# Rotary tables of two blocks in one VectorE operation, moved with the second residual ahead of the roots' seed

## The chip, the cores and the metric

The kernel runs on one core of a Trainium2 chip. The metric is the device time of one launch in microseconds. The engines are TensorE (PE, with its weight loads PEld), VectorE (DVE), ScalarE (ACT), GpSimd (POOL) and SyncE (SP), which issues the DMAs here. All data are float32.

## The reference, cut to what matters

The input is 2 x 1024 tokens of 128 features. A linear-attention layer comes first, then six layers of local attention and feed-forward, then a norm and a sum. The change lies in the attention of the six layers:

```python
x_in = shift_tokens(x)                         # half of the features come from the token before
q, k, v = split(x_in @ Wqkv[i])                # 16 heads of 64
q = l2norm(q) * q_scale[i];  k = l2norm(k) * k_scale[i]
q = q * cos * scale + rotate_half(q) * sin * scale
k = k * cos / scale + rotate_half(k) * sin / scale
x = local_attention(q, k, v) @ Wo[i] + x       # windows of 32, each sees itself and the one before
h = shift_tokens(x)
x = (a * gelu(gate)) @ W2[i] + b2[i] + x       # (a, gate) = layernorm(h) @ W1[i] + b1[i]
```

## The kernel before, in words

The tokens are cut into 16 blocks of 128 for each layer. Six layers make 96 blocks, worked off in 48 pairs (PAIRS); PPL = 8 pairs are a layer and PPB = 4 pairs one of the two sequences. Each engine has a function `step(m)` that is written out by hand and holds parts of the pairs m to m - 4: the projection of pair m, the attention of pair m - 1, the output projection of pair m - 2, the feed-forward norm of pair m - 3 and the feed-forward of pair m - 4. `run` (L707) writes out the first six steps (FILLED), loops over the steps 6 to 47 and writes out four more (BEHIND). So the order on each engine is fixed, and engines meet by semaphores that count up.

What VectorE does in a step (L1391 to L1433) for the pair's even block (u = 0) and odd block (u = 1):

- `tables` (L1276), once for each block at the step's begin: multiplies the cosines and sines of the block's positions (`rope`, 4 x 64 values for each token) by the layer's scales (`scales`) into `table[:, u]`, 256 elements, both inputs in SBUF.
- `turn_cos` (L1287) and `turn_sin` (L1298, two halves): multiply the projected q or k, in PSUM, by the table. They wait for the table (`tabled`) and for ScalarE's squares. GpSimd adds the two parts (L1456).
- `norm_square` (L1304), `mask` and `largest` (L1343, L1350), `sums` (L1356, L1358), `ff_gate` (L1377), `residual1` (L1364), `ff_norm` (L1371) between them.
- `find_roots` (L1307) near the end: inverse square roots of 64 head norms of q and k of both blocks and of two variances of the feed-forward norm. A first step (L1313 from the sums of squares, L1318 from the variances in PSUM), a seed by an integer operation on the bits (L1326, 67 elements), and three Newton rounds of three operations (L1330, L1333, L1336), each waiting for the one before.
- `residual2` (L1386) last: the feed-forward's output in PSUM, its bias and the kept sum `mid` into `xT`; it waits for `down_done` and signals `x_ready`.

GpSimd's order in a step (L1503): scale k of the even and q of the odd block of pair m - 1 by the roots (L1484), fold squares (L1469), scale k of the odd block, additions (L1456), subtraction of the row maxima (L1495), weighing by the inverted sums (L1500), a fold, the additions for q and k of the odd block, and last `scale_q` of the even block of pair m, which waits for the roots of the pair.

TensorE's order (L883) around the change: `ff_down` (L879) ends a step; the next one begins with transposes of probabilities (L786), a projection of q (L781), `ff_up` part 0 (L871, waits for `x_ready`), transposes of the even block's q (`turn_q`, L789 to L795, waits for `q_scaled`), the projection of k, transposes of k, `ff_up` part 1, transposes of the odd block's q (waits also for `q_turned`, the sines of the even block, as it writes the PSUM tile that they read), `ff_up` part 2 and the scores (L814). Later come the projections of v and q, the output projection (L839) and the rest.

```python
before = ROOT_OPS * m
dve.wait_ge(S["refined"], before + 2)
...
dve.tensor_scalar(root[:, :].bitcast(I32), minus_half[:, :].bitcast(I32), -0.5, GUESS,
                  ALU.mult, ALU.add).then_inc(S["refined"], 1)
```

Of the kernel before, what the change touches and what calls it, by code (L numbers as in the profile page):

```python
# [22 lines left out]
BPB = SEQ // P  # L23
NB = BATCH * BPB
# [3 lines left out]
PAIRS = STEPS // 2  # L28
PPL = NB // 2
PPB = BPB // 2  # L30
# [18 lines left out]
ROOT_OPS = 3 + 3 * NEWTON  # L49
# [5 lines left out]
def bcast(ap, axis, count):  # L55

    wide = ap.unsqueeze(axis)
    shape = list(wide.shape)
    shape[axis] = count
    return wide.broadcast_to(shape)  # L60
# [566 lines left out]
def layers(nc, weights, xT, ident, mean_w, center_w, eps):  # L627

    with ExitStack() as ctx:
        def sb(name, shape):  # L630
            return ctx.enter_context(nc.sbuf_tensor(name, shape, F32))

        def sem(name):
            return ctx.enter_context(nc.semaphore(name))
# [5 lines left out]
        window, rope, scales = weights.window, weights.rope, weights.scales  # L640


        table = sb("table", [P, 2, 4, DH])
# [48 lines left out]
        S = {name: sem(name) for name in names}  # L692
# [4 lines left out]
        LAG, FILLED, BEHIND = 2, 6, 4  # L697

        def runs(m):

            return not isinstance(m, int) or 0 <= m < PAIRS
# [2 lines left out]

            return isinstance(n, int) and n == 0

        def run(eng, step):  # L707

            for m in range(FILLED):
                step(m)  # L710
            with eng.Fori(FILLED, PAIRS) as m:
                step(m)
            for m in range(PAIRS, PAIRS + BEHIND):
                step(m)

        def pair_at(m):

            return (m % PPL) * W2 + (m % PPL) // PPB
# [552 lines left out]

        @block.vector
        def _(dve):
            def tables(n, u):

                dve.tensor_tensor(table[:, u, :, :].rearrange("p k d -> p (k d)"),  # L1276
                                  rope[:, bass.ds(n % BPB, 1), :, :].rearrange("p a k d -> p (a k d)"),
                                  scales[:, bass.ds(n // NB, 1), :, :].rearrange("p a k d -> p (a k d)"),
                                  ALU.mult).then_inc(S["tabled"], 1)

            def turn_cos(n, u, k, src, squared, turned, transposed):

                dve.wait_ge(S["tabled"], n + 1)
                dve.wait_ge(S[squared], n + 1)
                if not isinstance(n, int) or n >= 2:
                    dve.wait_ge(S[transposed], n - 1)
                dve.tensor_tensor(rot[:, u, k, :, :, :].rearrange("p h a d -> p h (a d)"),  # L1287
                                  src[:, :].rearrange("p (h d) -> p h d", h=HEADS),
                                  bcast(table[:, u, 2 * k, :], 1, HEADS), ALU.mult).then_inc(S[turned], 1)

            def turn_sin(n, u, k, src, turned, added):

                if not first(n):
                    dve.wait_ge(S[added], n)
                v = src[:, :].rearrange("p (h a d) -> p h a d", h=HEADS, a=2)
                for a in range(2):
                    sin = table[:, u, 2 * k + 1, 32 * a:32 * a + 32]
                    dve.tensor_tensor(rot_sin[:, k, :, a, :], v[:, :, 1 - a, :], bcast(sin, 1, HEADS),  # L1298
                                      ALU.mult).then_inc(S[turned], 1)
# [4 lines left out]
                dve.tensor_reduce(ss[:, (2 * u + k) * HEADS:(2 * u + k + 1) * HEADS], squares[:, k, :].rearrange("p (h a d) -> p h a d", h=HEADS, a=2)  # L1304
                                  [:, :, 0, :], AX.X, ALU.add).then_inc(S[summed], 1)

            def find_roots(m):  # L1307

                before = ROOT_OPS * m
                if runs(m):  # L1310
                    dve.wait_ge(S["q_summed"], 2 * (m + 1))
                    dve.wait_ge(S["k_summed"], 2 * (m + 1))
                    dve.tensor_scalar(minus_half[:, 0:QK_ROOTS + 1], ss[:, :],  # L1313
                                      1e-24, -0.5, ALU.max, ALU.mult)\
                       .then_inc(S["refined"], 1 if runs(m - LAG) else 2)
                if runs(m - LAG):
                    dve.wait_ge(S["var_done"], m - LAG + 1)
                    dve.tensor_scalar(minus_half[:, QK_ROOTS + 1:ROOTS], pm_norm[:, 0:2], 1e-5, -0.5, ALU.add, ALU.mult)\  # L1318
                       .then_inc(S["refined"], 1 if runs(m) else 2)
                dve.wait_ge(S["refined"], before + 2)  # L1320
                if runs(m - 1):
                    dve.wait_ge(S["q_scaled"], 2 * m)
                    dve.wait_ge(S["k_scaled"], 2 * m)
                if runs(m - LAG - 1):
                    dve.wait_ge(S["rstd_spread"], m - LAG)
                dve.tensor_scalar(root[:, :].bitcast(I32), minus_half[:, :].bitcast(I32), -0.5, GUESS,  # L1326
                                  ALU.mult, ALU.add).then_inc(S["refined"], 1)
                for i in range(NEWTON):
                    dve.wait_ge(S["refined"], before + 3 + 3 * i)
                    dve.tensor_tensor(root_t[:, :], minus_half[:, :], root[:, :], ALU.mult)\  # L1330
                       .then_inc(S["refined"], 1)
                    dve.wait_ge(S["refined"], before + 4 + 3 * i)
                    dve.tensor_tensor(root_t[:, :], root_t[:, :], root[:, :], ALU.mult)\  # L1333
                       .then_inc(S["refined"], 1)
                    dve.wait_ge(S["refined"], before + 5 + 3 * i)
                    dve.scalar_tensor_tensor(out=root[:, :], in0=root_t[:, :], scalar=1.5, in1=root[:, :],  # L1336
                                             op0=ALU.add, op1=ALU.mult).then_inc(S["refined"], 1)
# [44 lines left out]
            def residual2(m):  # L1382

                dve.wait_ge(S["down_done"], m + 1)
                at = pair_at(m) + 1
                dve.scalar_tensor_tensor(out=xT[:, bass.ds(at, W2)], in0=pm_norm[:, 0:W2],  # L1386
                                         scalar=cols[:, 2, bass.ds(m // PPL, 1)],
                                         in1=mid[:, bass.ds(at, W2)], op0=ALU.add, op1=ALU.add)\
                   .then_inc(S["x_ready"], 1)

            def step(m):  # L1391
                if runs(m):
                    tables(2 * m, 0)
                    tables(2 * m + 1, 1)
                    turn_cos(2 * m, 0, 0, r0, "q_squared", "q_turned", "qT_done")
                    turn_sin(2 * m, 0, 0, r0, "q_turned", "q_added")
                if runs(m - 4):
                    ff_gate(m - 4, 0, pm_norm)
                if runs(m):
                    turn_cos(2 * m, 0, 1, r1, "k_squared", "k_turned", "kT_done")  # L1400
                    turn_sin(2 * m, 0, 1, r1, "k_turned", "k_added")
                    norm_square(2 * m, 0, 0, "q_folded", "q_summed")
                if runs(m - 1):
                    mask(2 * m - 2, 0, r2)
                    largest(2 * m - 2, 0)
                if runs(m - 4):
                    ff_gate(m - 4, 1, pm_out)
                if runs(m - 1):
                    mask(2 * m - 1, 1, r0)
                    largest(2 * m - 1, 1)  # L1410
                    sums(2 * m - 2, 0)
                if runs(m - 4):
                    ff_gate(m - 4, 2, pm_norm)
                if runs(m):
                    norm_square(2 * m, 0, 1, "k_folded", "k_summed")
                    turn_cos(2 * m + 1, 1, 0, r1, "q_squared", "q_turned", "qT_done")
                    norm_square(2 * m + 1, 1, 0, "q_folded", "q_summed")
                if runs(m - 2):
                    residual1(m - 2)
                if runs(m - 1):  # L1420
                    sums(2 * m - 1, 1)
                if runs(m):
                    turn_sin(2 * m + 1, 1, 0, r1, "q_turned", "q_added")
                    turn_cos(2 * m + 1, 1, 1, r0, "k_squared", "k_turned", "kT_done")
                if runs(m - 3):
                    ff_norm(m - 3)
                if runs(m):
                    turn_sin(2 * m + 1, 1, 1, r0, "k_turned", "k_added")
                    norm_square(2 * m + 1, 1, 1, "k_folded", "k_summed")
                if runs(m) or runs(m - 2):  # L1430
                    find_roots(m)
                if runs(m - 4):
                    residual2(m - 4)  # L1433

            for b in range(BATCH):
                dve.memset(mid[:, b * (SEQ + 1):b * (SEQ + 1) + 1], 0.0)
# [3 lines left out]
            dve.wait_ge(S["cleared"], 1)  # L1440
            dve.wait_ge(S["tables_loaded"], 7 * 16)
            dve.sem_inc(S["x_ready"], PPL)
            run(dve, step)

        @block.gpsimd
        def _(pool):
# [206 lines left out]
```

## Time and profile before

| what | value |
|---|---|
| median of three runs | 1858.31 us (1854.05 to 1860.98) |
| the profiled execution | 1854.16 us, span 1852.3 us |
| mean granted TensorE clock | 0.972 |
| PE busy | 1673.8 us (90%) |
| DVE busy | 1562.0 us (84%) |
| POOL busy | 1488.4 us (80%) |
| ACT busy | 1219.1 us (66%) |
| tables (L1276) | 96 operations, 155.5 us |
| roots' seed (L1326) | 50 operations, 104.6 us |

The busy time of an engine says how much of the span it had an instruction running, also one that stood still behind something else. A timeline row has the start in us from the span's start, the duration, engine, line, operation, tiles and shapes; in brackets stands how long the engine had been idle before it, and what it had waited for. "x3" means that neighbouring instructions of one kind are merged. PEclk 1.00 is the full TensorE clock, 0.50 half of it.

### The profile page before, as it was taken

The page shows a single profiled execution, that of the slowest core. Times are in us where ns is not written, and L with a number is a line of the kernel's source. Part 1 is how long each engine was busy: PE and PEld are TensorE (multiplying, and loading weights), DVE is VectorE, ACT ScalarE, POOL GpSimd, SP SyncE. Part 2 cuts the span into 40 slices and gives each one's busy share as a digit, 9 for nine tenths or more (in the row PEclk, how much of TensorE's full clock was granted, in tenths as well). Part 3 has the DMA queues.
Part 4 walks back from the last instruction along what each step waited for, and adds up shares of the span by engine and source line. Part 5 has one row for each costly group of instructions (what it writes and reads, how often), then busy time and mean ns, then how long its engine had stood idle before and what let it go on. Part 6 is the DMA issues. An engine that isn't in the chain of part 4 may idle for free. (4 is left out here: it accounts for less than half of the span.)

```text
span 1852.3 us, 76505 instructions
## 1 busy us (share of the span) xinstructions
PE 1673.8 (90%) x30992; PEld 1195.4 (65%) x30992; DVE 1562.0 (84%) x2309; ACT 1219.1 (66%) x2072; POOL 1488.4 (80%) x823
## 2 busy tenths in 40 slices
PE   4957889899999999999999999999999999999985
PEld 3634566667667666676676676676666766766664
DVE  6878667898898898988989989988889989899853
ACT  3435455677777767767677777777677676777754
POOL 3568777788888888888888888888888888888851
PEclk7979889999999999999999999999999999999999
DMA  4002132121332221332212232222242223222220
GB/s 136 1 13 57 48 92 60 47 68 45 81 105 75 54 60 48 94 96 68 68 50 67 75 103 55 68 67 66 67 106 59 54 68 79 57 68 68 58 57 23
DMA packets 80697, 121.87 MB, mean 66 GB/s; under 512 B 16776, under 2 KB 29574, under 8 KB 79750
## 3 DMA queue, kind: packets, MB, share of 16 engines
q1 hardware_dynamic: 80646, 121.14, 24.9%
q8 instruction: 38, 0.62, 0.1%
q14 instruction: 13, 0.11, 0.0%
HBM read 19.36 MB, written 1.05 MB: 11 GB/s over the span
## 5 line engine op out<-in xcount | busy, mean ns | idle before, releaser
L781 PE MATMUL r<-wqkv,xs 128*128 (+1 forms) x1152 | 560.7, 618 | 13.4 <-DVE rot_sin L1298 4.3
L1484 POOL TENSOR_TENSOR rot<-rot,root 128x1024 f32<-128x1024 f32 x192 | 377.7, 1987 | 120.6 <-DVE root L1336 120.6
L1456 POOL TENSOR_TENSOR rot<-rot,rot_sin 128x1024 f32<-128x1024 f32 x192 | 451.8, 2364 | 1.6 <-DVE rot_sin L1298 1.6
L781 PEld LDWEIGHTS r<-wqkv,xs 128*128 128x128 f32 x1152 | 210.0, 195 | 213.4 <-issue 197.7
L1131 ACT ACTIVATE squares<-r 128x512 f32<-128x512 f32 x384 | 217.6, 598 | 80.5 <-PE r L781 79.3
L1287 DVE TENSOR_TENSOR rot<-r,table 128x1024 f32<-128x1024 f32 x192 | 232.8, 1213 | 21.0 <-PE r L786 9.6
L1469 POOL TENSOR_TENSOR squares<-squares 128x512 f32<-128x512 f32 x192 | 244.5, 1273 | 6.6 <-ACT squares L1131 6.5
L1500 POOL TENSOR_TENSOR probs<-probs,rinv 128x1024 f32<-128x1024 f32 x96 | 182.7, 1903 | 81.2 <-DVE rinv L1358 81.2
L1298 DVE TENSOR_TENSOR rot_sin<-r,table 128x512 f32<-128x512 f32 x384 | 242.6, 673 | 0.0
L786 PE MATMUL r<-square,rot 128*128 128x128 f32 x1536 | 208.4, 279 | 17.3 <-POOL rot L1484 11.8
L786 PEld LDWEIGHTS r<-square,rot 128*128 128x128 f32 x1536 | 169.5, 141 | 81.2 <-issue 27.5
L1495 POOL TENSOR_TENSOR sm<-sm,rowmax 128x1024 f32<-128x1024 f32 x96 | 182.6, 1902 | 45.4 <-DVE rowmax L1350 45.1
L1343 DVE TENSOR_TENSOR sm<-r,window 128x1024 f32<-128x1024 f32 x96 | 117.6, 1225 | 109.6 <-PE r L814 109.6
L1166 ACT ACTIVATE qT<-r 128x1024 f32<-128x1024 f32 x96 | 98.2, 1023 | 165.6 <-PE r L786 165.6
L871 PE MATMUL pm<-xn,w 128*128 128x256 f32 (+1 forms) x576 | 153.4, 390 | 58.4 <-DVE xT L1386 57.8
L830 PE MATMUL r<-pT,vwin 64*64 64x32 f32 x12288 | 202.9, 221 | 2.6 <-issue 2.6
L830 PEld LDWEIGHTS r<-pT,vwin 64*64 64x64 f32 x12288 | 191.7, 137 | 13.5 <-issue 12.9
L839 PE MATMUL pm<-attnT,wo 128*128 128x256 f32 x768 | 175.5, 382 | 1.2 <-issue 1.2
L839 PEld LDWEIGHTS pm<-attnT,wo 128*128 128x128 f32 x768 | 147.0, 192 | 41.2 <-issue 23.3
L1276 DVE TENSOR_TENSOR table<-rope,scales 128x256 f32 (+1 forms) x96 | 155.5, 1658 | 10.2 <-issue 10.1
L871 PEld LDWEIGHTS pm<-xn,w 128*128 128x128 f32 (+1 forms) x576 | 93.9, 180 | 107.7 <-issue 87.0
L1116 ACT ACTIVATE kT<-r 128x1024 f32<-128x1024 f32 x96 | 98.3, 1024 | 96.6 <-PE r L786 91.4
(123 smaller groups left out, 2723.2 us busy)
## 6 DMA issues: line engine op xcount, KB each, us to landing
vwin<-vtok SPq DMA_DIRECT2D x576, 128.0 KB, 2.3
vwin<-vtok SPq DMA_DIRECT2D x384, 64.0 KB, 2.0
wqkv<-in_wqkv SPq DMA_DIRECT2D x6, 1536.0 KB, 8.3
wo<-in_wo SPq DMA_DIRECT2D x6, 512.0 KB, 4.9
w<-in_w SPq DMA_DIRECT2D x6, 341.0 KB, 2.9
x<-in_x SPq DMA_DIRECT2D x4, 256.0 KB, 3.6
rope<-in_rope SPq DMA_DIRECT2D x1, 1024.0 KB
out_x<-y SPq DMA_DIRECT2D x4, 256.0 KB, 2.3
```

What stands on the lines that cost most here:

```text
L781: pe.matmul(dst[:, c * 512:(c + 1) * 512], xs1[:, u, :], w.rearrange("p a n -> p (a n)"), start=True, stop=True).then_inc(S[done], 1)
L786: last = pe.transpose(dst[:, f * P:(f + 1) * P], src[:, f * P:(f + 1) * P], ident)
L830: last = pe.matmul(dst[DH * s:DH * (s + 1), at + WIN * w:at + WIN * (w + 1)], vwin[half, u, w, 2 * i + s, :], pT[half, u, (FT // 2) * s + ...
L839: last = pe.matmul(pm_out[:, 0:W2], wo[:, f, :], attnT[:, (f % 2) * (FT // 2) + f // 2, :], start=(f == 0), stop=(f == FT - 1))
L871: last = pe.matmul(dst[0:rows, half * W2:(half + 1) * W2], w1[:, half * FF + at:half * FF + at + rows], xn2[:, :], start=True, stop=True)
L1131: last = act.activation(squares[:, k, c * 512:(c + 1) * 512], src[:, c * 512:(c + 1) * 512], ACT.Square)
L1287: dve.tensor_tensor(rot[:, u, k, :, :, :].rearrange("p h a d -> p h (a d)"), src[:, :].rearrange("p (h d) -> p h d", h=HEADS), bcast(table ...
L1298: dve.tensor_tensor(rot_sin[:, k, :, a, :], v[:, :, 1 - a, :], bcast(sin, 1, HEADS), ALU.mult).then_inc(S[turned], 1)
L1456: pool.tensor_tensor(r, r, rot_sin[:, k, :, :, :].rearrange("p h a d -> p h (a d)"), ALU.add)\
L1469: pool.tensor_tensor(halves[:, :, 0, :], halves[:, :, 0, :], halves[:, :, 1, :], ALU.add)\
L1484: pool.tensor_tensor(r, r, bcast(root[:, at:at + HEADS], 2, DH), ALU.mult)\
L1500: pool.tensor_tensor(probs[:, u, :, :], probs[:, u, :, :], bcast(rinv[:, u, :], 2, 2 * WIN), ALU.mult)\
```

## The change

`tables` is no longer called once for each block but once for each pair, in a single operation over both blocks (2 x 256 elements; the scales are read twice through a repeated axis). It is called one pair ahead: `tables(0)` before the first step, `tables(m + 1)` in step m, behind the roots' first step. `find_roots` is cut in two, `begin_roots` (L1313, L1318) and `finish_roots` (the seed and the Newton rounds). Between the two stand now the tables of the next pair and then `residual2`, which stood behind all of the roots. The count of `tabled` goes up by one for each pair, and its waits are halved accordingly. The last looped step of VectorE is written out, since it has no next pair.

```diff
-        def run(eng, step):
+        def run(eng, step, end=PAIRS):
             for m in range(FILLED):
                 step(m)
-            with eng.Fori(FILLED, PAIRS) as m:
+            with eng.Fori(FILLED, end) as m:
                 step(m)
-            for m in range(PAIRS, PAIRS + BEHIND):
+            for m in range(end, PAIRS + BEHIND):
                 step(m)
...
-            def tables(n, u):
-                dve.tensor_tensor(table[:, u, :, :].rearrange("p k d -> p (k d)"),
-                                  rope[:, bass.ds(n % BPB, 1), :, :].rearrange("p a k d -> p (a k d)"),
-                                  scales[:, bass.ds(n // NB, 1), :, :].rearrange("p a k d -> p (a k d)"),
+            def tables(m):
+                dve.tensor_tensor(table[:, :, :, :].rearrange("p u k d -> p u (k d)"),
+                                  rope[:, bass.ds((m % PPB) * 2, 2), :, :].rearrange("p a k d -> p a (k d)"),
+                                  bcast(scales[:, bass.ds(m // PPL, 1), :, :].rearrange("p a k d -> p (a k d)"), 1, 2),
                                   ALU.mult).then_inc(S["tabled"], 1)
             def turn_cos(n, u, k, src, squared, turned, transposed):
-                dve.wait_ge(S["tabled"], n + 1)
+                dve.wait_ge(S["tabled"], n // 2 + 1)
...
-            def find_roots(m):
+            def begin_roots(m):
...
+            def finish_roots(m):
+                before = ROOT_OPS * m
                 dve.wait_ge(S["refined"], before + 2)
...
             def step(m):
                 if runs(m):
-                    tables(2 * m, 0)
-                    tables(2 * m + 1, 1)
                     turn_cos(2 * m, 0, 0, r0, "q_squared", "q_turned", "qT_done")
...
                 if runs(m) or runs(m - 2):
-                    find_roots(m)
+                    begin_roots(m)
+                if runs(m + 1):
+                    tables(m + 1)
                 if runs(m - 4):
                     residual2(m - 4)
+                if runs(m) or runs(m - 2):
+                    finish_roots(m)
...
-            run(dve, step)
+            tables(0)
+            run(dve, step, PAIRS - 1)
```

## Rows read from the trace of the kernel before

**Rows 1.** The page, busy us (share of the span) and instructions

```profile
PE 1673.8 (90%) x30992; PEld 1195.4 (65%) x30992; DVE 1562.0 (84%) x2309; ACT 1219.1 (66%) x2072; POOL 1488.4 (80%) x823
```

**Rows 2.** Busy times by stretch: us, each engine's busy us, PEclk, DMA share, GB/s

```profile
344.48:1777.00 1432.52, 1355.15 (x26335) 978.99 (x26336) 1273.26 (x1841) 1011.17 (x1670) 1237.06 (x669) 1.00 0.27 69
```

**Rows 3.** Timeline of GpSimd, one step of the steady part

```profile
911.87 1.90 POOL L1500 TENSOR_TENSOR probs<-probs,rinv 128x1024 f32<-128x1024 f32 x1 [1.73 <-DVE rinv L1358]
...
914.96 4.68 POOL L1456 TENSOR_TENSOR rot<-rot,rot_sin 128x1024 f32<-128x1024 f32 x2
922.14 5.99 POOL L1484 TENSOR_TENSOR rot<-rot,root 128x1024 f32<-128x1024 f32 x3 [2.50 <-DVE root L1336]
...
945.99 1.90 POOL L1500 TENSOR_TENSOR probs<-probs,rinv 128x1024 f32<-128x1024 f32 x1 [1.73 <-DVE rinv L1358]
```

**Rows 4.** Timeline of VectorE, the same step

```profile
916.28 1.10 DVE L1313 TENSOR_SCALAR minus_half<-ss 128x65 f32<-128x65 f32 x1
917.30 0.14 DVE L1318 TENSOR_SCALAR minus_half<-pm 128x2 f32<-128x2 f32 x1
917.48 2.21 DVE L1326 TENSOR_SCALAR root<-minus_half 128x67 int32<-128x67 int32 x1
...
921.83 0.23 DVE L1336 SCALAR_TENSOR_TENSOR root<-root_t,root 128x67 f32<-128x67 f32 x1
922.30 0.49 DVE L1386 SCALAR_TENSOR_TENSOR xT<-pm,cols,mid 128x256 f32 x1 [0.24 <-issue]
923.02 3.34 DVE L1276 TENSOR_TENSOR table<-rope,scales 128x256 f32 x2 [0.24 <-issue]
...
927.42 1.27 DVE L1298 TENSOR_TENSOR rot_sin<-r,table 128x512 f32<-128x512 f32 x2
...
944.07 0.42 DVE L1364 TENSOR_TENSOR mid<-pm,xT 128x256 f32 x1 [0.72 <-PE pm L839]
```

**Rows 5.** Instructions of two lines: duration ns min/median/max, first and last start

```profile
L1326 DVE TENSOR_SCALAR root<-minus_half x50: 195/2212/2287, 141.4 to 1820.5; 128x67 int32<-128x67 int32 x50
...
L1276 DVE TENSOR_TENSOR table<-rope,scales x96: 416/2015/2123, 119.8 to 1743.7; 128x256 f32 x84, 128x256 f32<-128x256 f32 x12
```

**Rows 6.** Timeline of TensorE and its weight loads, the same step

```profile
918.64 0.60 PE L879 MATMUL pm<-hid,w 85*128 85x256 f32 x2
...
923.08 1.12 PE L871 MATMUL pm<-xn,w 128*128 128x256 f32 x4 [1.25 <-DVE xT L1386]
924.09 1.09 PE L786 MATMUL r<-square,rot 128*128 128x128 f32 x8
...
927.61 1.03 PE L871 MATMUL pm<-xn,w 128*128 128x256 f32 x4
928.75 1.09 PE L786 MATMUL r<-square,rot 128*128 128x128 f32 x8
...
928.75 0.85 PEld L786 LDWEIGHTS r<-square,rot 128*128 128x128 f32 x8 [0.51 <-DVE rot_sin L1298]
```

**Rows 7.** Timeline of VectorE ahead of the steady part

```profile
102.65 0.69 DVE L190 TENSOR_TENSOR o<-o,ln_rstd 128x512 f32<-128x512 f32 x1
...
119.80 0.76 DVE L1276 TENSOR_TENSOR table<-rope,scales 128x256 f32<-128x256 f32 x2 [0.18 <-DVE minus_half L1439]
```

**Rows 8.** Timeline of TensorE behind gaps; last row: busy us and PEclk of a stretch

```profile
136.61 3.65 PE L781 MATMUL r<-wqkv,xs 128*128 128x512 f32 x4 [2.51 <-DVE rot_sin L1298]
...
259.34 1.64 PE L786 MATMUL r<-square,rot 128*128 128x128 f32 x8 [2.35 <-POOL rot L1484]
...
1776.36 1.13 PE L871 MATMUL pm<-xn,w 128*128 128x256 f32 x4 [2.72 <-DVE xT L1386]
...
1791.80 0.45 PE L814 MATMUL r<-kT,qT 64*32 64x64 f32 x28 [1.92 <-issue]
...
259.67:263.08 3.41, 3.41 (x10) 0.50 0.18 59
```

## The prediction

> **What bounds the kernel now.** I read the page's busy times first. TensorE is busy 90% of the span and VectorE 84% [rows 1]: both near a bound, so only order can tell which one. The busy times by stretch show that the steady part, where the granted clock is 1.00 throughout, takes most of the span, with 1355 us of TensorE and 1273 us of VectorE in 1432.5 us [rows 2]. The same operation of GpSimd comes back after 945.99 - 911.87 = 34.12 us [rows 3], which is the length of one step (one pair of blocks).
>
> Next the timelines of one step, to find the chain that closes on itself. VectorE takes the roots' first step at 916.28, reads the variance, and issues the seed at 917.48. The seed takes 2.21 us for 67 elements and ends at 919.69 [rows 4]; it has taken as little as 195 ns [rows 5]. What ends it is on GpSimd: the second of two additions (4.68 us from 914.96) ends at 919.64 [rows 3]. So an operation of VectorE out of SBUF waits for the running one of GpSimd. The first step's 1.10 us ends at 917.38 in the same way, where the first addition ends. The tables are the third case: 416 ns at least, 2015 in the median [rows 5], while GpSimd scales q and k [rows 3, 4]. Operations with a PSUM input in the same places do not wait (the second residual takes 0.49) [rows 4]. After the seed come nine short operations, and the roots are ready at 922.06, which starts GpSimd's scaling at 922.14 [rows 3, 4].
>
> From there two branches lead to TensorE's transposes of q of the odd block (928.75). On one, GpSimd's scaling of q releases the transposes of the even block at 924.09, and TensorE works on through projection, transposes of k and second up-projection until 927.61 + 1.03 = 928.64 [rows 6]. On the other, VectorE runs the second residual, two tables (3.34 us), cosine and sines; the sines end at 927.42 + 1.27 = 928.69 [rows 4]. The second branch is last: the weight load of those transposes waited 0.51 us for the sines [rows 6]. Then TensorE works without a gap to the output projection, which releases the first residual at 944.07; the sums behind it release GpSimd's weighing at 945.99, which had idled 1.73 us [rows 3, 4]. The weighing, a fold and the two additions end at the next 953.8, where the next seed gets through. So the circle is: roots, residual, tables, rotation, TensorE, first residual, GpSimd, roots.
>
> **The change part by part.** Durations are of the profiled execution: 1854.16 us with a span of 1852.3. The median of the three runs is 4 us more, so a change of the sum is to be added to either; a measurement of this kernel can tell about 0.5%, some 9 us.
>
> *Removed from the second branch:* two tables, 3.34 us and the 0.24 us of issue ahead of them [rows 4], and the residual, which now stands ahead of the seed. This branch ends about 2.9 us earlier. It stops being the last one.
>
> *Added ahead of the seed: one tables operation over 512 elements.* It has two SBUF inputs, and GpSimd's addition runs from 917.3 to 919.64, so it waits as the seed did. Alone, 512 elements take 0.69 us [rows 7] against the seed's 0.20; the seed ended 0.05 after GpSimd, so the tables end 0.05 + 0.49 after it, at 920.18. Lowest bound: it does not wait and costs the roots nothing. Highest: 0.69, and 0.24 of issue that I take to be hidden under the wait. I take 0.49, because the seed in the same place is the nearest row.
>
> *Moved ahead of the seed: the second residual*, 0.49 less the 0.08 by which neighbours overlap (916.28 + 1.10 against 917.30) [rows 4], so 0.40. Its input is ready: the down-projection ends at 918.64 + 0.60 = 919.24 [rows 6]. What waits behind it on VectorE is the seed and all nine operations, and for them GpSimd's scaling.
>
> *The seed itself* meets an idle GpSimd: 0.20, less 0.08. The roots end 0.49 + 0.40 + 0.12 = 1.01 us later, at 923.07.
>
> *The first branch* therefore starts 1.01 later: transposes at 925.10. Until 928.75 it had a slack of 0.22 (928.64 less an overlap of 0.11, as between 923.08 + 1.12 and 924.09) [rows 6]; the weight load's 0.51 would be the most. Each step becomes 1.01 - 0.22 = 0.79 us longer, with ends at 0.50 and at 1.03 (with the issue time). 41 steps (6 to 46) have tables, residual and roots together: 41 x 0.79 = 32 us. In the steps 1 to 5 before them, tables alone cost three times 0.49 and both twice 1.01: 3 us. In the last steps the tables are gone and I count nothing; the lone residual of step 47 would be 0.4. The tables before the loop replace two of 0.76 together [rows 7] under a wait for projections: nothing. Waits on the halved count of tables are one per turning operation, as now.
>
> *The residual earlier* lets TensorE's first up-projection start at 921.83 instead of 923.08 [rows 6], closing its largest gap of 1.25. This earns nothing, since the transposes behind it wait for GpSimd. But it makes one long gap, from about 922.8 to 925.1: 2.3 us. Is the clock kept? In the filling stage a gap of 2.35 us before 259.34 was followed by 3.41 us at half the clock (granted 0.50, the 1.2 GHz level), eight transposes taking 1.64 instead of 1.09; a gap of 2.72 before 1776.36 was not followed by any fall [rows 8, 6]. Of the twelve gaps over 1.9 us that began at full clock (the first before 136.61, the last before 1791.80 [rows 8]) ten were followed by a fall. So a fall can come in none to ten twelfths of the steps. I take two in five, nearer to the lower end, because the gaps in the filling stage have others near them and in the steady step the rest is closed. One fall costs between 3.41 x (1 - 1.09/1.64) = 1.15 and half of 3.41, 1.7; I take 1.5. 41 x 0.4 x 1.5 = 25 us.
>
> **Sum:** 1854 + 32 + 3 + 25 = 1914 us. Without any fall of the clock 1889, and with the small end 0.50 also 1875; with ten twelfths at 1.7 and 1.03 a step, 1854 + 42 + 5 + 58 = 1959.
>
> **A rule that says otherwise.** The rows show the price of an operation of its own: two tables without a neighbour take 0.76 us, one of 512 elements 0.69 [rows 7]. The Trainium skill ("VectorE: DVE Perf Modes", Rules for kernel authors) advises to keep the number of operations low. By that rule alone the step would gain 0.07 us and the time would be 1854 - 3 = 1851; it is the first rival's price within 2 us. The Trainium skill ("SBUF — State Buffer", Who interferes with whom) speaks against the change: a VectorE operation with two SBUF inputs and a GpSimd one that reads SBUF exclude each other for a whole instruction. The trace agrees with it by the ends at 919.69 and 919.64.
>
> **The rivals.** 1. *The tables disappear in the wait (no change).* If the new form with a repeated operand does not wait for GpSimd, it runs from about 917.7 to 918.4, the residual follows the down-projection from 919.28, and the seed ends near 919.9: roots 0.2 later, slack 0.22, nothing gained or lost, 1853. For it: there are 2 us of waiting to hide in. Against: every table beside a busy GpSimd took about 2 us.
> 2. *The same, and faster.* The point that decides is TensorE's slack at 928.75. If the roots come 0.2 later and the slack is the weight load's 0.51, the removed tables give 0.30 us a step: 1854 - 12 = 1842. Against: it needs both the missing wait and the larger slack.
> 3. *No fall of the clock*: the first branch late by 0.79 a step, 1889. For it: the steady steps kept the clock through a gap of 1.25. Against: ten gaps of twelve.
> 4. *The tables are not one operation but two on the chip*, or registers must be worked out in the open: 0.1 to 0.24 more a step, up to 1924. That changes no sign.
>
> **How the numbers follow.** Forecast with falls 0.52, no or hardly any falls 0.34, rival 1 0.09, rival 2 0.05. The own range of the forecast is 1896 to 1945. The range reaches down to 1872, to hold the case without falls with its small end, and up to 1942; left out are rivals 1 and 2 (0.14) and the extreme of falls. Slower by over 0.5% is 0.86, within 0.5% 0.09, faster 0.05.
>
> **What would show it.** Tables x48 with a median near 2.7 us, ending about 0.5 us after GpSimd's second addition; the seed at 0.2 us; GpSimd idle before its scaling for 3.5 us instead of 2.5; a wait of TensorE's transposes for GpSimd's scaling of some 2.3 us in each step, and none for the sines; the step at 34.9 us, and 36.4 where the clock fell. Wrong if the tables take 0.7 us with GpSimd busy, if the step stays under 34.3, or if the granted clock in the steady part stays at 1.00 (then 1889 is the number).

## The result, and the profile after

The changed kernel takes 1922.93 us in the median (1922.15 to 1924.15, four runs), the kernel before beside it 1856.18 us (1852.77 to 1860.98). The ratio is 1.0358, with a 95% interval of 1.0332 to 1.0385: 3.6% slower. The forecast was 1914 us with a range of 1872 to 1942. The profiled run took 1922.95 us, with a span of 1921.1 and a mean granted clock of 0.953 (before: 0.972).

The page's busy times of the changed kernel; they answer to [rows 1]:

```profile
PE 1692.4 (88%) x30992; PEld 1217.9 (63%) x30992; DVE 1437.3 (75%) x2261; ACT 1222.6 (64%) x2072; POOL 1471.9 (77%) x823
```

VectorE has 125 us less to do than before, and the share of every engine fell. A shorter busy time on an engine is no gain by itself: the kernel waits more now. VectorE's timeline of one step shows where, beside [rows 4]:

```profile
944.78 1.09 DVE L1313 TENSOR_SCALAR minus_half<-ss 128x65 f32<-128x65 f32 x1
945.79 0.15 DVE L1318 TENSOR_SCALAR minus_half<-pm 128x2 f32<-128x2 f32 x1
945.86 2.82 DVE L1276 TENSOR_TENSOR table<-rope,scales 128x512 f32 x1
948.60 0.47 DVE L1389 SCALAR_TENSOR_TENSOR xT<-pm,cols,mid 128x256 f32 x1
949.00 0.18 DVE L1329 TENSOR_SCALAR root<-minus_half 128x67 int32<-128x67 int32 x1
...
951.32 0.23 DVE L1339 SCALAR_TENSOR_TENSOR root<-root_t,root 128x67 f32<-128x67 f32 x1
954.71 1.22 DVE L1287 TENSOR_TENSOR rot<-r,table 128x1024 f32<-128x1024 f32 x1 [3.16 <-PE r L786]
```

And GpSimd's timeline of the same step, beside [rows 3]; the two additions are the second row, the scaling the third:

```profile
940.36 1.90 POOL L1506 TENSOR_TENSOR probs<-probs,rinv 128x1024 f32<-128x1024 f32 x1 [1.76 <-DVE rinv L1361]
943.46 4.67 POOL L1462 TENSOR_TENSOR rot<-rot,rot_sin 128x1024 f32<-128x1024 f32 x2
951.63 5.62 POOL L1490 TENSOR_TENSOR rot<-rot,root 128x1024 f32<-128x1024 f32 x3 [3.49 <-DVE root L1339]
975.17 1.91 POOL L1506 TENSOR_TENSOR probs<-probs,rinv 128x1024 f32<-128x1024 f32 x1 [1.76 <-DVE rinv L1361]
```

Read both by their distance from the end of the additions (943.46 + 4.67 = 948.13). The tables end 0.55 after it (948.68), the seed takes 0.18, the roots end at 951.55, 3.42 after it. Before, the same distance was 922.06 - 919.64 = 2.42. So the roots come 1.00 us later, and GpSimd idles 3.49 us ahead of its scaling where it idled 2.50. The step is 975.17 - 940.36 = 34.81 us, 0.69 longer than the 34.12 of [rows 3].

The instructions of the two lines whose order was changed, beside [rows 5]: the seed never meets GpSimd any more, the tables nearly always do.

```profile
L1276 DVE TENSOR_TENSOR table<-rope,scales x48: 680/2821/2887, 119.2 to 1798.7; 128x512 f32 x41, 128x512 f32<-128x512 f32 x7
...
L1329 DVE TENSOR_SCALAR root<-minus_half x50: 179/180/186, 141.3 to 1888.5; 128x67 int32<-128x67 int32 x50
```

TensorE's timeline, beside [rows 6]; the last two rows are one step later:

```profile
950.16 1.03 PE L871 MATMUL pm<-xn,w 128*128 128x256 f32 x4
953.58 1.09 PE L786 MATMUL r<-square,rot 128*128 128x128 f32 x8 [2.40 <-POOL rot L1490]
954.51 1.88 PE L781 MATMUL r<-wqkv,xs 128*128 x4
...
988.39 1.24 PE L786 MATMUL r<-square,rot 128*128 128x128 f32 x8 [2.39 <-POOL rot L1490]
989.43 3.47 PE L781 MATMUL r<-wqkv,xs 128*128 x4
```

The gap is the same in both steps, but the projection behind it takes 1.88 us in one and 3.47 in the other. The table of windows explains it (columns: window, its us, PE's busy us with the count, granted clock, DMA share, GB/s):

```profile
381.44:1801.81 1420.37, 1309.08 (x25122) 0.98 0.26 67
953.29:956.70 3.41, 3.12 (x17) 1.00 0.14 41
988.91:992.33 3.42, 3.42 (x10) 0.54 0.00 0
```

In the second of these steps TensorE was granted 0.54, nearly the 1.2 GHz level. Of the 40 steps between the seeds of steps 6 and 46, 16 have such a fall and take 36.50 us instead of 34.81 (medians), so 1.69 us for each. These 40 steps took 1365.66 us before and 1420.37 now, and 40 x 0.69 + 16 x 1.69 = 54.7 is all of the difference. Of the 68.8 us between the two profiled runs, 7.2 more lie in the filling stage and 6.9 at the end, if both kernels are cut where GpSimd's additions of steps 6 and 46 end. (The seeds of step 6 are 10.2 apart, 371.24 and 381.44, because the seed used to be issued ahead of that end and to wait, and now comes behind it.)

The view of waits tells the same (us in total, times, longest): GpSimd's waits for the roots grew from 120.6 to 165.7 us, and TensorE's 119.8 us for the scaling of q are new in this place.

```profile
PE r L786 <- POOL rot L1490: 119.8, 48, 3.9
```

### The profile page after: what moved, and what is told of

It is laid out like the page before. It is cut to its first block and busy times, and to the rows that moved or that the text cites. A ratio compares the mean times of both kernels' runs of the same rounds, so it can differ in the third digit from the quotient of the medians.

```text
span 1921.1 us, 76425 instructions
## 1 busy us (share of the span) xinstructions
PE 1692.4 (88%) x30992; PEld 1217.9 (63%) x30992; DVE 1437.3 (75%) x2261; ACT 1222.6 (64%) x2072; POOL 1471.9 (77%) x823
## 5 line engine op out<-in xcount | busy, mean ns | idle before, releaser
L781 PE MATMUL r<-wqkv,xs 128*128 (+1 forms) x1152 | 587.6, 643 | 13.5 <-DVE rot_sin L1298 4.2
L1490 POOL TENSOR_TENSOR rot<-rot,root 128x1024 f32<-128x1024 f32 x192 | 361.0, 1901 | 165.7 <-DVE root L1339 165.7
L781 PEld LDWEIGHTS r<-wqkv,xs 128*128 128x128 f32 x1152 | 216.9, 202 | 221.3 <-issue 205.7
L786 PE MATMUL r<-square,rot 128*128 128x128 f32 x1536 | 212.6, 283 | 120.9 <-POOL rot L1490 119.8
L786 PEld LDWEIGHTS r<-square,rot 128*128 128x128 f32 x1536 | 180.5, 146 | 186.9 <-POOL rot L1490 117.6
L814 PE MATMUL r<-kT,qT 64*32 64x64 f32 x12288 | 146.9, 227 | 17.5 <-issue 17.5
L871 PE MATMUL pm<-xn,w 128*128 128x256 f32 (+1 forms) x576 | 152.8, 391 | 2.0 <-DVE xT L1389 1.2
L814 PEld LDWEIGHTS r<-kT,qT 64*32 64x32 f32 x12288 | 129.7, 106 | 38.3 <-issue 36.3
```

The lines of the kernel that those rows point to most:

```text
L781: pe.matmul(dst[:, c * 512:(c + 1) * 512], xs1[:, u, :], w.rearrange("p a n -> p (a n)"), start=True, stop=True).then_inc(S[done], 1)
L786: last = pe.transpose(dst[:, f * P:(f + 1) * P], src[:, f * P:(f + 1) * P], ident)
L814: last = pe.matmul(dst[rows, at:at + 2 * WIN], qT[half, u, f, rows], kT[half, u, f, WIN * w:WIN * (w + 2)], start=True, stop=True)
L1490: pool.tensor_tensor(r, r, bcast(root[:, at:at + HEADS], 2, DH), ALU.mult)\
```

## The experiments

The theory on trial: the tables are exposed by 0.5 us and the residual by 0.4 behind the end of GpSimd's addition, all of which delays the roots; the branch through VectorE, which the change shortens, has a spare of only 0.3; and the longer gap on TensorE costs clock. "Step" below is the usual distance of two seeds without a fall of the clock: the median, to 0.01 us, of the 40 distances between steps 6 and 46. Falls are counted in the profiled run. A run's kernel before was measured beside it (1857.88 to 1860.40 us in the median).

**1. One table operation, where the two stood (from the kernel before).**

```diff
... (tables and its waits as in the change)
                 if runs(m):
-                    tables(2 * m, 0)
-                    tables(2 * m + 1, 1)
+                    tables(m)
```

> Only the fusion: one tables operation for the pair at the place where the two stood, behind the roots and the second residual; nothing else moved. Two-branch theory: the tables wait for GpSimd's scaling of q until 924.05 and end 0.55 later, 924.6 instead of 926.36, so VectorE's branch is no longer the last one; the branch over GpSimd and TensorE (slack 0.30, as the changed kernel showed: roots 1.00 later, step 0.69 longer) then sets the step: 33.8 us instead of 34.12, 1854 - 13 = 1841 us. Rival, that the step follows VectorE's own work: 1.75 us a step, about 1775 us. Rival, that the fusion itself costs: not below 1854.

Measured: 1845.31 us (1842.78 to 1850.64), ratio 0.9915 [0.989, 0.994]; step 33.81, no falls. VectorE's timeline:

```profile
922.93 1.55 DVE L1276 TENSOR_TENSOR table<-rope,scales 128x512 f32 x1 [0.24 <-issue]
925.12 1.22 DVE L1287 TENSOR_TENSOR rot<-r,table 128x1024 f32<-128x1024 f32 x1 [0.64 <-PE r L786]
```

The tables take 1.55 where they took 3.34, so this branch is 1.79 shorter, and the cosine waits for TensorE now. The step gains only 0.31: that is the spare between the branches. The 1.79 are for the most part one wait for GpSimd saved and not work: alone, the two tables take 0.76 together [rows 7] and the single one 0.68. Fusing is good by itself; the loss lies in the moves.

**2. and 3. One move alone.** Run 2 is the changed kernel with the residual back behind the roots; run 3 is the kernel before with only the residual ahead of the seed.

```diff
# 2, from the changed kernel
                 if runs(m + 1):
                     tables(m + 1)
-                if runs(m - 4):
-                    residual2(m - 4)
                 if runs(m) or runs(m - 2):
                     finish_roots(m)
+                if runs(m - 4):
+                    residual2(m - 4)
# 3, from the kernel before
                 if runs(m) or runs(m - 2):
-                    find_roots(m)
+                    begin_roots(m)
                 if runs(m - 4):
                     residual2(m - 4)
+                if runs(m) or runs(m - 2):
+                    finish_roots(m)
```

> The fused tables between the roots' first step and the seed, one pair ahead, but the second residual stays behind the roots. Two-branch theory: roots 0.60 later (the tables' 0.55 behind GpSimd and a bare seed), step 0.30 longer, 34.4 us; with 5 us in the filling stage 1871 us if the clock holds. TensorE's gap ahead of the first up-projection grows from 1.25 to about 1.85; if that is enough for falls of the clock, up to 1890. If instead the position of the tables is the whole cost and the residual is free: near the changed kernel, 1915 or more.

Measured: 1887.2 us (1882.12 to 1887.34), ratio 1.0145 [1.012, 1.0169]; step 34.42, TensorE's gap 1.84, 7 falls in 40. The roots end 3.02 behind the additions instead of 2.42, and the step is 0.30 longer, as the theory has it (0.60 less 0.31, within 0.01); with the falls, the time is at the upper end of what was expected.

> Only the second residual moved ahead of the seed; two tables at their old place. Theory: it runs while the seed would wait for GpSimd anyway (from 919.3 to 919.8), roots 0.2 later, VectorE's branch 0.5 shorter, the other 0.1 below today's: 1849 us, 1845 to 1853; TensorE's gap is then about 1.5 and the clock holds. If the residual costs its full 0.40 on the roots: 1858. If the earlier residual is what brings the falls of the clock: over 1865, with a granted clock under 1 in the steady part.

Measured: 1902.84 us (1898.37 to 1908.04), ratio 1.0221 [1.0193, 1.0248]; step 34.74, gap 2.02, 13 falls in 40. The theory missed this by 54 us. VectorE's timeline:

```profile
942.33 0.49 DVE L1389 SCALAR_TENSOR_TENSOR xT<-pm,cols,mid 128x256 f32 x1 [2.26 <-PE pm L879]
...
945.77 3.83 DVE L1276 TENSOR_TENSOR table<-rope,scales 128x256 f32 x2 [0.47 <-issue]
```

and TensorE's and GpSimd's of the same step:

```profile
940.30 1.56 PE L879 MATMUL pm<-hid,w 128*128 128x256 f32 x6 [0.29 <-DVE minus_half L1318]
...
947.33 0.88 PE L786 MATMUL r<-square,rot 128*128 128x128 f32 x6 [2.02 <-POOL rot L1489]
```

```profile
937.58 4.69 POOL L1461 TENSOR_TENSOR rot<-rot,rot_sin 128x1024 f32<-128x1024 f32 x2
945.38 5.99 POOL L1489 TENSOR_TENSOR rot<-rot,root 128x1024 f32<-128x1024 f32 x3 [3.11 <-DVE root L1339]
```

The down-projection ends at 941.86, but the residual starts at 942.33, after GpSimd's additions have ended (942.27). I take the 0.47 between for instructions without a busy time, such as VectorE shows as "issue", which stand behind the wait here and so in the open. No row names them, but in step 47 of the changed kernel, which is written out and not looped, the residual starts only 0.04 after the down-projection (1834.97 and 1835.01). The residual therefore finds no shadow, and the roots come 0.61 later (945.30 - 942.27 = 3.03 against 2.42). The shorter VectorE branch that I expected to pay for it isn't shorter either: the tables end 4.30 after the roots in both kernels, since the second ends 0.28 after GpSimd's second scaling in both (949.60 and 949.32 here, 926.36 and 926.08 before), whatever time it starts.

**4. The changed kernel with the residual first, then the tables.**

```diff
-                if runs(m + 1):
-                    tables(m + 1)
                 if runs(m - 4):
                     residual2(m - 4)
+                if runs(m + 1):
+                    tables(m + 1)
```

> The changed kernel with its two moved operations in the other order: residual, then tables. Theory: the residual (an input in PSUM) does not wait for GpSimd and runs in the shadow, the tables start at its end when GpSimd is just done: roots 0.8 later than in the kernel before instead of 1.0; step 34.6, falls of the clock in about two of five steps as in the changed kernel: 1915 us. If the order of the two does not matter: 1923.

Measured: 1936.37 us (1932.51 to 1939.2), ratio 1.041 [1.038, 1.044]; step 35.01, gap 2.60, 20 falls in 40: slower than the changed kernel where it was expected faster. VectorE:

```profile
953.72 0.48 DVE L1389 SCALAR_TENSOR_TENSOR xT<-pm,cols,mid 128x256 f32 x1 [2.26 <-PE pm L879]
954.12 0.68 DVE L1276 TENSOR_TENSOR table<-rope,scales 128x512 f32 x1
```

The residual waits as in run 3, and the tables come behind it at their full price of 0.68. In the changed kernel the tables' wait for GpSimd hides the residual's wait for the down-projection and its issue (947.73 + 0.47 = 948.20, and the tables end at 948.68); that is why the two moves together cost 0.69 and not 0.30 + 0.62.

**5. Roots whose inputs stand in PSUM (from the kernel before).** If the wait for GpSimd is the price, take away its cause: with `minus_half` and `root_t` in free columns of `pm_out`, no operation of the roots has two SBUF inputs, and none goes from SBUF to SBUF. The first step also waits for ScalarE's squares of the centred block, which read this PSUM tile last, and it is now done in every step, so that these columns are always written before the seed reads them.

```diff
-        minus_half = sb("minus_half", [P, ROOTS])
-        root_t = sb("root_t", [P, ROOTS])
...
+        minus_half, root_t = pm_out[:, 256:256 + ROOTS], pm_out[:, 384:384 + ROOTS]
...
+                if runs(m - 2):
+                    dve.wait_ge(S["xc_squared"], m - 1)
```

> The kernel before, with the roots' two helper tiles (minus_half, root_t) in free columns of PSUM instead of SBUF, so that no operation of the roots has two SBUF inputs and none goes from SBUF to SBUF; order unchanged (the first step also waits for ScalarE's squares of the centred block). Theory that these operations wait for GpSimd because of where their operands lie: first step and seed take about 0.2 us each instead of 1.10 and 2.21, the roots end at about GpSimd's last addition instead of 2.4 us behind it, GpSimd scales without a pause, TensorE's gap of 1.25 us closes, step 32.7 to 33.0 and the bound then TensorE: 1858 - 42 x 1.2 = about 1808 us. Rival, that an operation of VectorE waits for GpSimd wherever its operands lie, or that the integer form is simply slow: 1858 or, with slower PSUM operands, up to 1875.

Measured: 1745.83 us (1742.72 to 1749.41), ratio 0.9386 [0.9362, 0.9411]: 6.1% faster than the kernel before, and the best of all. VectorE, GpSimd, TensorE, and a window of the steady part (us, then each engine's busy us, clock, DMA share, GB/s):

```profile
899.96 0.23 DVE L1314 TENSOR_SCALAR pm<-ss 128x65 f32<-128x65 f32 x1
...
900.40 0.23 DVE L1327 TENSOR_SCALAR root<-pm 128x67 int32<-128x67 int32 x1
...
902.82 0.23 DVE L1337 SCALAR_TENSOR_TENSOR root<-pm,root 128x67 f32<-128x67 f32 x1
```

```profile
898.64 4.68 POOL L1457 TENSOR_TENSOR rot<-rot,rot_sin 128x1024 f32<-128x1024 f32 x2
903.28 5.99 POOL L1485 TENSOR_TENSOR rot<-rot,root 128x1024 f32<-128x1024 f32 x3
```

```profile
904.99 1.03 PE L870 MATMUL pm<-xn,w 128*128 128x256 f32 x4
905.85 1.04 PE L785 MATMUL r<-square,rot 128*128 128x128 f32 x8
```

```profile
344.48:1677.00 1332.52, 1327.07 (x26089) 988.23 (x26090) 1156.49 (x1835) 1005.88 (x1665) 1233.64 (x667) 1.00 0.28 74
```

The roots run beside GpSimd's additions and are done at 903.05, before these end (903.32). GpSimd goes on to scale without a pause, TensorE has no gap, and the step is 31.83 us, with TensorE busy in 99.6% of the window. The same two operations that took 1.10 + 2.21 us in [rows 4] take 0.46 here, so nearly all of the rest was waiting. The mechanism was as expected, the gain 62 us larger.

**6. The same with the fused tables of run 1.**

> The same with the fused tables at the old place. If TensorE is the bound once the roots no longer wait, nothing more to gain: within 4 us of the kernel with the roots in PSUM alone. If VectorE's branch is still last: another 0.3 to 1 us a step, 12 to 40 us.

Measured: 1746.6 us (1743.64 to 1748.64), ratio 0.94 [0.9375, 0.9424]; step 31.84. Nothing is left to gain there: TensorE is the bound.

**7. Only the gap filled (from the changed kernel).** Eight transposes of the identity, whose results nobody reads, follow the first up-projection.

```diff
+                    if runs(m - 4):
+                        for f in range(FT):
+                            pe.transpose(r2[:, f * P:(f + 1) * P], ident, ident)
```

> The changed kernel with eight more transposes (of a constant, into the PSUM tile that the real ones overwrite) on TensorE behind the first up-projection, in the steps from 4 on: they do no useful work and fill 0.95 us of the 2.4 us gap. Theory, that the falls of the granted clock come from the gap: no step of 36.5 any more, all 34.8, 1923 - 16 x 1.7 = 1896 us and a little less in the filling stage. If the falls have another cause: 1923. If the added transposes delay the real ones: over 1923.

Measured: 1881.97 us (1880.32 to 1884.49), ratio 1.0121 [1.0097, 1.0146]. TensorE's timeline, and the window that answers to [rows 2]:

```profile
932.17 1.04 PE L938 MATMUL r<-square 128*128 128x128 f32 x8
934.74 0.44 PE L786 MATMUL r<-square,rot 128*128 128x128 f32 x2 [1.53 <-POOL rot L1493]
```

```profile
344.48:1777.00 1432.52, 1351.64 (x26089) 1006.19 (x26089) 1141.19 (x1765) 994.26 (x1642) 1201.68 (x657) 1.00 0.26 68
```

Every steady step takes 34.79 to 34.91 us and the clock stays at 1.00. Useless work thus gives back 41 of the change's 67 us, 14 more than expected. Between the two profiled runs it is 38.4: 27.1 in the steady part, 8.5 in the filling stage (the seed of step 6 is at 372.90 us instead of 381.44) and 2.8 at the end. What stays, 24 us against the kernel before beside it, is in the main the later roots.

**8. The whole change on top of run 5.** TensorE's second up-projection also waits for the roots in the last steps, since it writes the same PSUM tile; the rest is the change as it stands.

```diff
+                    if isinstance(m, int) and PAIRS < m < PAIRS + 3:
+                        pe.wait_ge(S["refined"], ROOT_OPS * m)
                     ff_up(m - 4, 1, pm_out)
```

> The whole change and the roots' helper tiles in PSUM together. Theory: the tables keep two SBUF inputs, wait for GpSimd's second addition ahead of the seed as before, and hold back roots that no longer wait themselves: roots 3.4 to 3.7 us behind the addition, step 34.8 to 35.1 with falls of the clock, 1920 to 1940 us, so that the change now costs 10% against the kernel with the roots in PSUM alone. Rival, that the roots' own operations were what waited and the tables pass: below 1780.

Measured: 1857.19 us (1853.56 to 1862.17, ten runs), ratio 0.9997 [0.9982, 1.0012]. The change costs 6.4% on this base (1857.19 against 1745.83), but the time is 60 to 80 us under the expectation. VectorE and GpSimd, and TensorE:

```profile
908.10 0.23 DVE L1316 TENSOR_SCALAR pm<-ss 128x65 f32<-128x65 f32 x1
...
908.50 1.20 DVE L1277 TENSOR_TENSOR table<-rope,scales 128x512 f32 x1
911.17 0.48 DVE L1392 SCALAR_TENSOR_TENSOR xT<-pm,cols,mid 128x256 f32 x1 [1.48 <-PE pm L878]
```

```profile
906.77 5.14 POOL L1465 TENSOR_TENSOR rot<-rot,rot_sin 128x1024 f32<-128x1024 f32 x2
```

```profile
909.13 1.56 PE L878 MATMUL pm<-hid,w 128*128 128x256 f32 x6
...
916.23 0.99 PE L785 MATMUL r<-square,rot 128*128 128x128 f32 x7 [2.08 <-POOL rot L1493]
```

With the first step no longer held up, the tables are issued during the first addition (which ends at 909.14), pass between the two (they end at 909.70, the two additions take 5.14 together instead of 4.68) and cost little. Then the residual waits for the down-projection (ends 910.69) in the open, as in run 3. The step is 34.13, and in spite of a gap of 2.08 there is no fall in 40 steps.

**9. Only `minus_half` in PSUM (from the kernel before).** Which operations wait? Here the products `root_t` x `root` keep two SBUF inputs, everything else has one.

```diff
+        minus_half = pm_out[:, 256:256 + ROOTS]
+        root_t = sb("root_t", [P, ROOTS])
```

> The kernel before with only minus_half in PSUM: first step, seed and the first product have at most one SBUF input and none goes from SBUF to SBUF, the second product (root_t times root) has two SBUF inputs. Theory, that a product of two SBUF inputs waits for GpSimd as the first step and the seed did: the second product waits for the end of the additions, roots about 2.0 us behind them instead of 2.4, step 33.6 to 33.8, 1838 to 1848 us. Rival, that only operations from SBUF to SBUF with one tensor input wait: as with both tiles in PSUM, 1746.

Measured: 1825.45 us (1815.75 to 1826.16), ratio 0.981 [0.9775, 0.9844]; step 33.42.

```profile
905.32 0.23 DVE L1335 TENSOR_TENSOR root_t<-root_t,root 128x67 f32<-128x67 f32 x1
905.59 2.27 DVE L1338 SCALAR_TENSOR_TENSOR root<-root_t,root 128x67 f32<-128x67 f32 x1
```

```profile
903.04 4.73 POOL L1458 TENSOR_TENSOR rot<-rot,rot_sin 128x1024 f32<-128x1024 f32 x2
```

The first operation with two SBUF inputs came just where one addition gives way to the next (905.41) and took 0.23; the next took 2.27 and ended at 907.86, the additions at 907.77. So an operation with two SBUF inputs waits too, not only the seed's form, and the rival theory for this run (a time of run 5's size) falls. The time is 13 us below the 1838 to 1848 expected: the roots end 1.66 behind the additions and not 2.0.

**10. Run 8 with the residual behind the roots.**

```diff
-                if runs(m - 4):
-                    residual2(m - 4)
                 if runs(m) or runs(m - 2):
                     finish_roots(m)
+                if runs(m - 4):
+                    residual2(m - 4)
```

> Helper tiles in PSUM and the tables moved ahead of the seed, the second residual left behind the roots. Theory: what the whole change costs on top of the PSUM roots (1746 to 1857 us) is mostly the residual, which waits for the down-projection and its registers in front of the seed; the tables slip in between GpSimd's two additions (VectorE passes at once behind the first, the second starts 0.46 later). Roots and scaling then come 0.7 to 0.9 later than with PSUM alone, of which TensorE's slack of about 0.66 hides most: step 31.9 to 32.2, 1746 to 1762 us. Rival, that the tables' wait is what costs: step 34, near 1857.

Measured: 1762.17 us (1758.53 to 1763.97), ratio 0.9489 [0.9472, 0.9506]; step 32.18, at the upper end of what was expected. The tables pass between the additions as in run 8:

```profile
934.92 1.19 DVE L1277 TENSOR_TENSOR table<-rope,scales 128x512 f32 x1
```

Between runs 5 and 8 lie 111 us; moving the tables takes 16 of them, moving the residual 95.

TensorE's largest gap in a steady step, with the falls that followed. It lies ahead of q's transposes; in the kernel before and runs 1, 2 and 9 ahead of the first up-projection.

| kernel | gap, us | falls in 40 steps |
|---|---|---|
| runs 5, 6, 10 | about 0.1 | 0 |
| run 9 | 0.90 | 0 |
| before; run 1 | 1.25 | 0 |
| run 7 | 1.53 | 0 |
| run 2 | 1.84 | 7 |
| run 3 | 2.02 | 13 |
| run 8 | 2.08 | 0 |
| changed | 2.39 to 2.40 | 16 |
| run 4 | 2.60 | 20 |

## Why the prediction was right

**Tables (0.54 behind the addition): right**, 0.55 by the timeline; the wait ends with GpSimd's instruction, as for the seed in [rows 4]. Two of the readings behind it were wrong. "An operation of VectorE out of SBUF waits" is too wide: the sum of the norm squares (L1304), SBUF to SBUF with one input, takes 0.68 us at 915.50, in the midst of the first addition (914.96 to 917.33), and does not wait. And the ends at 919.69 and 919.64 belong to the seed, which has a single SBUF input, so they are no case of the rule for two; such cases are the tables and run 9's second product (907.86 and 907.77). What the Trainium skill ("SBUF — State Buffer", Who interferes with whom) says of operations with at most one SBUF input, that they don't contend with GpSimd outside the modes with two ports, agrees with runs 5 and 9: the seed takes 0.23 beside a running addition when its input is in PSUM. From SBUF it takes 2.21; no row shows which mode it then runs in.

**Residual (0.40) and seed (0.12): right as a sum**, 1.00 us for the roots against 1.01. The reason I gave was weak, though. "Its input is ready" holds only since the tables' wait covers the down-projection and the issue time; runs 3, 4 and 8 show it in the open where that cover is gone.

**The first branch's slack (0.22): too small.** It is 1.00 - 0.69 = 0.31, and run 1 gives the same 0.31 from the other side. I had taken an overlap of 0.11 between projection and transposes; where the two follow each other freely in run 5 it is 904.99 + 1.03 - 905.85 = 0.17, which alone makes 0.28. So a step is 0.69 longer and not 0.79: 28 us of 40 steps instead of 32.

**"This branch ends about 2.9 us earlier": right in that it is no longer the last, and worth nothing.** The cosine now idles 3.16 us for TensorE; the 2.9 itself can't be read off. Run 3 adds that it holds only with the fused tables: two separate ones end with GpSimd's second scaling.

**Falls of the clock (two in five at 1.5 us): right**, 16 in 40 at 1.69, or 27 us. Run 7 shows them as a cause: filled gaps, no falls, and 1882 us, near the 1889 of rival 3. That the share came out exact is luck, for the grounds for two in five were thin. The steady part's share could not be worked out from the filling stage's, and run 8 (2.08, none) says that the length of the gap alone doesn't decide.

**Filling stage (3 us) and end (nothing): too small**, 7.2 and 6.9. At the end it is in the main the clock, for which I had a term in the steady part alone; in the filling stage the clock has a part. The windows of TensorE (window, its us, PE's busy us, granted clock, DMA share, GB/s), before and changed: first the steps 5 and 6, then all from the seed of step 46 to the end.

```profile
292.50:371.24 78.74, 69.06 (x1256) 0.96 0.22 56
294.10:381.44 87.34, 73.84 (x1257) 0.88 0.20 50
...
1736.90:1852.30 115.40, 86.00 (x1490) 0.95 0.18 47
1801.80:1921.10 119.30, 88.66 (x1476) 0.87 0.17 44
```

Run 7, with its gaps filled, has steps 5 and 6 in 76.9 us at 0.98, so that the 8.6 us which these two steps lost are mostly clock. The steps 1 to 4 had a higher clock than before, though (0.91 over 152.8 us, before 0.88 over 151.1), so the 7.2 of the whole stage can't be divided between clock and later roots by these rows. At the end, the lone residual of step 47 does wait for the down-projection, but the roots come only 0.17 later for it (2.59 behind the additions instead of 2.42). It releases the up-projection early, so that TensorE's waits, 2.72 us and 0.22 before, become one gap of 3.38 us, behind which the transposes run at about half the clock:

```profile
1835.01 0.48 DVE L1389 SCALAR_TENSOR_TENSOR xT<-pm,cols,mid 128x256 f32<-128x256 f32 x1 [1.83 <-PE pm L879]
```

```profile
1840.08 1.94 PE L786 MATMUL r<-square,rot 128*128 128x128 f32 x8 [3.38 <-POOL rot L1490]
```

The sum came out 9 us low: -4 from the slack, +2 from the falls, +11 from filling and end. Rival 1 (tables that vanish) and rival 2 (and faster) fall with the tables' 2.82 us; rival 4 falls too, with one operation and no issue time in its row. The rule of few operations ("VectorE: DVE Perf Modes" in the Trainium skill, Rules for kernel authors) holds in run 1, where it brought 15 us, though through a wait saved and not through the price of an operation; in the changed kernel it is outweighed by where the operation stands.

## What to carry to other kernels

Ahead of an operation that a slower engine waits for, only such work is free as ends within a wait that is there anyway; ask of each moved operation not only when its input is ready, but where its own wait and its issue would lie if the cover went. Before shifting work into a wait, look for the wait's cause: two operands of 67 columns moved to PSUM took away all of it and brought 6.1%, where the cleverer order lost 3.6%. Gaps on TensorE can cost twice, when the clock falls behind them, so price them by the stage's own rows and test them by filling them.

## What was not expected of the hardware

- An operation of VectorE that waits for GpSimd gets through between two queued instructions of GpSimd, and the next one of these then comes later: in run 8 the tables took 1.20 us, and the two additions 5.14 instead of 4.68.
- A small integer operation from SBUF to SBUF with a single input, the seed, takes 2.21 us beside an addition, 0.18 to 0.20 alone, and 0.23 beside it with its input in PSUM; a product with two SBUF inputs waits in the same way (2.27), and a sum over one SBUF input does not (0.68).
- Gaps of 1.84 to 2.60 us are followed by a fall of TensorE's clock to about half in 7 to 20 of 40 steps at 1.4 to 1.7 us each, but one of 2.08 in no step of run 8. What made that difference was not found out.
- Between the end of what the residual waits for and its start lie 0.47 us in the looped steps (runs 3 and 8) and 0.04 in step 47, which is written out. I take the difference for instructions without a busy time; behind a semaphore's wait it is paid in full.
